# Products of a tile of ones, read by nothing, ahead of 55 waits of TensorE in a four-layer network on one core

## The reference

```python
xn = _layernorm(x, axis=-1)
x = x + _L0_attn_ref(xn, ...) + _L0_ffn_ref(xn, ...)   # causal attention, 16 heads; ternary weights
xn = _layernorm(x, axis=-1)
x = x + _L1_attn_ref(xn, ...) + _L1_ffn_ref(xn, ...)   # gated recurrence; 16 experts, top 2, + shared
xn = _layernorm(x, axis=-1)
x = x + _L2_attn_ref(xn, ...) + _L2_ffn_ref(xn, ...)   # one head of 256; weights from a spline
xn = _layernorm(x, axis=-1)
x = x + _L3_attn_ref(xn, ...) + _L3_ffn_ref(xn, ...)   # rotary attention, 16 heads; 8 experts, top 2
return x
```

## Time and profile before

| | |
|---|---|
| median of 3 runs | 1212.69 us (1212.25 to 1215.65) |
| the profiled execution's own time | 1219.58 us |
| its span, first to last instruction | 1218.0 us |
| PE busy | 1096.1 us, 90% of the span |
| mean granted clock of TensorE | 0.951 |

### The profile page before, as it was taken

One profiled execution on the slowest core, in us unless ns is written; L12 is line 12 of the kernel. 1 busy time (PEld: TensorE's weight loads), 2 busy tenths in 40 slices (PEclk: granted clock), 3 DMA queues, 4 the chain that ended last, 5 costly groups with the idle time before them and its releaser, 6 DMA issues.

```text
span 1218.0 us, 17428 instructions
## 1 busy us (share of the span) xinstructions
PE 1096.1 (90%) x6542; PEld 720.0 (59%) x6556; DVE 841.0 (69%) x1602; ACT 641.5 (53%) x980; POOL 498.2 (41%) x549
## 2 busy tenths in 40 slices
PE   3698999999999888999579999999699998997998
PEld 2466686766665454674257998989234543553445
DVE  6985856678568897955767435267877679668751
ACT  6644647466569885642135333242187166465473
POOL 4864748375524526411774052244231331141131
PEclk9778999999999999998789999999799989998999
DMA  7724344324340101267370000006914526425320
GB/s 216 214 55 146 87 129 149 116 79 142 94 174 35 36 1 48 70 198 229 106 75 27 1 1 1 1 10 159 217 38 122 140 55 149 101 67 155 92 72 18
DMA packets 86116, 116.42 MB, mean 96 GB/s; under 512 B 29617, under 2 KB 43281, under 8 KB 85265
## 3 DMA queue, kind: packets, MB, share of 16 engines
q1 hardware_dynamic: 47792, 70.28, 19.2%
q0 software_dynamic: 38240, 45.03, 15.1%
HBM read 81.54 MB, written 40.40 MB: 100 GB/s over the span
## 4 chain that ended last, share of the span: by engine, by line
PE 61%; DVE 14%; ACT 7%; POOL 6%; issue 6%; DMA 5%; SPq 1%; ACTq 0%; DVEq 0%; POOLq 0%
PE pair L693 23%; PE bank L693 18%; PE bank L772 6%; PE pair L762 5%; PE pair L751 4%; DVE max L1157 3%; POOL gathered L2092 2%; ACT probs L1681 2%; DMA h<-comb 1%; PE pair L712 1%; PE bank L780 1%; SPq L2124 1%; POOL h L2110 1%; PE pair L792 1%; DMA kept<-q_low 1%
## 5 line engine op out<-in xcount | busy, mean ns | idle before, releaser
L1157 DVE TENSOR_REDUCE max<-pair 128x2 f32<-128x1024 f32 (+3 forms) x256 | 252.5, 1021 | 61.7 <-PE pair L742 32.1
L1681 ACT ACTIVATE probs<-pair 128x1024 f32<-128x1024 f32 (+3 forms) x256 | 212.5, 865 | 103.3 <-PE pair L762 85.6
L751 PE MATMUL pair<-ks,qs 64*128 64x512 f32 (+3 forms) x512 | 110.6, 456 | 24.4 <-DVE max L1157 10.8
L2013 POOL TENSOR_TENSOR h_low<-hidden,h_high 128x512 fp32r<-128x512 f32 x64 | 82.8, 1299 | 97.8 <-ACT h_high L1719 97.3
L772 PE MATMUL bank<-probs,v 128*32 128x512 f32 (+3 forms) x1024 | 115.4, 536 | 1.1 <-POOL probs L2057 0.5
L762 PE MATMUL pair<-qs,ks 64*128 64x512 f32 (+3 forms) x512 | 102.1, 435 | 13.3 <-DVE max L1157 5.1
L751 PEld LDWEIGHTS pair<-ks,qs 64*128 64x128 f32 x512 | 50.4, 199 | 80.3 <-DVE max L1157 31.5
L762 PEld LDWEIGHTS pair<-qs,ks 64*128 64x128 f32 x512 | 46.2, 190 | 76.7 <-ACT probs L1681 24.5
L1713 ACT ACTIVATE hidden<-pair 128x512 f32<-128x512 f32 x64 | 38.2, 599 | 80.9 <-PE pair L693 69.9
L2110 POOL TENSOR_TENSOR h<-mix_h,h 128x512 bf16<-128x512 f32 x48 | 54.9, 1172 | 57.4 <-DMA h<-comb 39.1
L1196 DVE TENSOR_TENSOR x<-bank,x 128x512 f32<-128x512 f32 x32 | 22.0, 688 | 80.2 <-PE bank L693 80.1
(11 more groups left out here) (330 smaller groups left out, 2673.9 us busy)
## 6 DMA issues: line engine op xcount, KB each, us to landing
kept<-q_high SPq DMA_DIRECT2D x64, 256.0 KB, 3.8
qs<-kept POOLq DMA_DIRECT2D x32, 512.0 KB, 4.1
ks<-kept POOLq DMA_DIRECT2D x32, 512.0 KB, 5.2
kept<-q_low SPq DMA_DIRECT2D x32, 256.0 KB, 4.1
expert_in<-in_experts_in SPq DMA_DIRECT2D x16, 352.0 KB, 4.1
expert_out<-in_experts_out SPq DMA_DIRECT2D x16, 256.0 KB, 5.5
h<-comb SPq DMA_DIRECT2D x4, 1024.0 KB, 5.5
tern_raw<-in_ffn_in SPq DMA_DIRECT2D x8, 256.0 KB, 6.6
```

Of the source, the lines that this page charges most:

```text
L751: made = mm(to[:, hh, 0:n], m.qs[k][slot][r0:r0 + STACK, p, qt * P:(qt + 1) * P], m.ks[k][slot][r0:r0 + STACK, p, 0:n], start=True, stop=k ...
L1157: V.tensor_reduce(m.max[:, g % 2, :, p, qt], to[:, :, 0:n], AX.X, ALU.max).then_inc(*s.done("top"))
L1681: A.activation(m.probs[(2 * kt + p) % 4][:, :, q0:T], to[:, :, q0:T], ACT.Exp, scale=0.25).then_inc(*s.done("exp"))
L2013: Q.tensor_tensor(m.h_low[k][:, j, :], m.hidden[k][j % 2][:, :], m.h_high[k][:, j, :].bitcast(F32), ALU.subtract).then_inc(*s.done("low"))
```

## The change

Two new kinds of PE step are put between the others. A `warm` step writes a pair, a `hum` step one bank. Each does 4 times n products of 128 columns, `ones16` by `ones16`, into PSUM, and nothing reads them: 35 groups with 197 x 4 products and 20 with 72 x 4, together 1076. A group waits until its banks are free as every step does, and then for nothing else (ones16 has long been there). `DUE` gets new numbers, since every inserted step shifts those behind it, but the order of all other steps on all five engines stays the same, and so do their banks.

```diff
+WARM = (11, 4, 5, 9, 11, 3, 4, 1, 1, 3, 7, 4, 1, 1, 2, 39, 6, 8, 7, 1, 3, 3, 2, 9, 8, 3, 10, 7, 3, 3, 3, 4, 6, 4, 1,)
+HUM = (5, 5, 9, 5, 2, 6, 5, 1, 4, 4, 5, 2, 2, 5, 2, 4, 1, 2, 2, 1,)
...
 PARTS = {
     "PE": {
+        "warm": keys(range(len(WARM))), "hum": keys(range(len(HUM))),
...
+    "warm": "2 11 15 18 21 74 468 473 487 492 502 568 571 575 597 604 606 732 736 742 744 749 752 754 757 846 849 859 861 864 866 869 873 1030 1049",
+    "hum": "6 13 71 465 475 490 601 705 707 710 714 718 720 722 725 1035 1039 1043 1047 1058",
...
-BANKS = {"tern_sum": "pair",
+BANKS = {"warm": "pair", "hum": "one", "tern_sum": "pair",
...
+    "warm": "00400402044424400442442444240204400",
+    "hum": "66767667777777777776",
...
+    "warm": lambda n: [], "hum": lambda n: [],
...
+    def warm(n):
+
+        to = bank("warm", n)
+        pe.wait_ge(*at("set_dve", 0))
+        for i in range(4 * WARM[n]):
+            made = mm(to[:, 0, i % 4 * P:(i % 4 + 1) * P], m.ones16[:, :], m.ones16[:, :], start=True, stop=True)
+        made.then_inc(*s.done("warm"))
+
+    def hum(n):
+
+        to = bank("hum", n)
+        pe.wait_ge(*at("set_dve", 0))
+        for i in range(4 * HUM[n]):
+            made = mm(to[:, i % 4 * P:(i % 4 + 1) * P], m.ones16[:, :], m.ones16[:, :], start=True, stop=True)
+        made.then_inc(*s.done("hum"))
```

More of the change, by code:

```diff
@@ L291 @@
 JOINT = {name: joint for joint, names in {
+    "idle_pe": ("warm", "hum"),
     "route_pe": ("count", "logit_turn"),
@@ L305 @@
           "gates1": 2, "rest1": 3, "qkv2": 1, "small3": 2, "bias3": 3, "qkv3": 2, "wo3": 1, "shared3": 2}
-BANKS = {"tern_sum": "pair", "turn": "pair", "qk": "pair", "vals": "pair", "score": "pair", "prob": "pair", "weigh": "acc", "back": "one",
+BANKS = {"warm": "pair", "hum": "one", "tern_sum": "pair", "turn": "pair", "qk": "pair", "vals": "pair", "score": "pair", "prob": "pair", "weigh": "acc", "back": "one",
          "rows": "pair", "unit": "pair", "down": "one", "mean": "one", "proj": "pair", "gate": "two", "gamma": "pair", "inflow_turn": "pair", "mem_turn": "two",
@@ L1022, in mix @@
         made.then_inc(*s.done("mix"))
-    parts = {"tern_sum": tern_sum, "turn": turn_x, "qk": qk, "vals": vals, "score": score, "prob": prob, "weigh": weigh, "back": back, "rows": rows, "out": out,
+    parts = {"warm": warm, "hum": hum, "tern_sum": tern_sum, "turn": turn_x, "qk": qk, "vals": vals, "score": score, "prob": prob, "weigh": weigh, "back": back, "rows": rows, "out": out,
              "unit": unit, "down": down, "mean": mean, "proj": proj, "gate": gate, "gamma": gamma, "inflow_turn": inflow_turn, "mem_turn": mem_turn, "shared": shared,
```

## The result

The change makes the kernel slower: 1225.61 us (median of 20 executions, 1219.99 to 1233.39) against 1216.96 us for the kernel before on the same chip (20 executions, 1209.89 to 1224.72). The ratio is 1.0073, 95% interval 1.0053 to 1.0093, so +8.9 us with 6.5 to 11.3. The three executions of before that the prediction knew, with a median of 1212.69, are the first of its 20. The profiled execution of after has a span of 1225.5 us, 7.5 more than before's 1218.0, and nearly the whole median difference can be followed in this pair of traces.

What follows compares the result with a forecast made beforehand. PE's work plus its waits was taken to bound the kernel; -11.9 us from A, B, D, E, F and J and +9.6 from H and I gave -2.3, so 1212.69 would become 1210.4 us, range 1203.5 to 1219.0.

Steps and rivals of the forecast that it cites:

- H: From mix (0, 4) to back (3, 0, 0): products outside the wait, partly given back by clock and waits; +5.6 us.
- I: From back (3, 0, 0) to turn (3, 2): 8.4 us of products, partly given back by clock and idle time; +4.0 us.
- rival of ones without effect: Products of ones do nothing for the clock and nothing comes back: about +18 us, 1231 us; chance 0.04.
- slower rival: Nothing of H, I and J lies in a wait: +7.6 us, 1220.3 us; chance 0.18.
- J: From turn (3, 2) to the end: products mostly in waits, DVE limits the gain from the clock; -1.2 us.
- A: Start to score (0, 0, 2, 0, 3): faster transposes, then DVE sets the time and covers PE; -0.3 us.
- G: From turn (2, 3) to mix (0, 4): DVE is busy with row maxima, so faster scores only wait; 0.
- B: Up to back (0, 0, 1): products fit the wait for row maxima and PE's low-clock work shortens; -2.3 us.
- E: Up to merge (0): 10.20 us of low-clock work halves and the gathers start earlier; -4.7 us.
- C: Between back (0, 0, 1) and expert_out (3), ahead of D: ACT is busy and hides PE; 0.
- D: Up to expert_out (3): products fit two waits and two low-clock windows full of PE work shorten; -3.1 us.
- F: From merge (0) to turn (2, 3): 156 products fill half a wait, the clock falls again under the gathers; -0.3 us.

Runs made afterwards that it cites:

- k1: The kernel before with its 32 indirect gathers as plain reads of the same bytes (result not the network's): 1213.52 us, ratio 0.9936.
- e3: The whole change, but each of the 16 groups of H and I has 4 products in place of 4 to 40: 1226.67 us, ratio 1.0012 to before.
- e1: The change without the 320 products of H and I, the other 39 groups kept: 1221.80 us, ratio 0.9976 to the kernel before.
- e2: Only the 320 products of H and I, none of the change's other 39 groups: 1241.51 us, ratio 1.0131 to the kernel before.
- h1: The kernel before, unchanged, run again for a profile: 1229.49 us, one execution.
- g2: The change without H, I and the 156 products ahead of the transposes of turn (2, 0): 1217.42 us, ratio 0.9934 to the kernel before.
- h2: g2 also without warm 1 to 4, 116 products where DVE sets the time: 1220.14 us, ratio 0.9974 to the kernel before.
- h4: h2 with group I, 156 products, put back: 1229.18 us, ratio 1.0045 to the kernel before.

## Why the prediction was wrong

**The clock came as forecast; the price of the ones in H and I was too low.** Products of ones do raise the clock (0.951 to 0.983, "about 0.98" was forecast), at 0.056 us each (0.054). The Trainium skill, "TensorE: Matmul & The Clock Gate", section "Wait — 56ns, not 53.3ns?", gives about 62 ns per MATMUL where the sequencer's own program decodes it, and 55.6 ns from start to start for products of 128 columns at the full clock. The trace's 0.0559 us agrees with the second, and no run here shows the first. The Trainium skill, same page, Part 1, has activity release the throttle; the mean clock of 0.983 agrees, even for products that nothing reads. The rival of ones without effect is out. The forecast of -2.3 became +7.5 in the pair. Of the 15.2 us between 1210.4 and the 1225.61 measured, 4.3 are the base: the median of the kernel before is 1216.96 over 20 executions, where the first three had 1212.69. The slower rival had +7.6, by the mechanism that the traces show ("nothing of H, I and J lies in a wait"), and I gave it 0.18. That its number meets the pair's is luck: it had 18.3 for H, I and J and -10.7 for the rest, and the pair has 14.4 and -6.9.

**I: +4.0 forecast, +7.9 measured** (8.7, 9.0 and 10.3 in the other pairs). Two terms of the step failed. The first is "where PE is idle for 2.3 us", half of it taken as room for products. It is mostly waits of 0.84, 0.53 and 0.55 us for DVE and ACT (timeline of PE, before):

```profile
977.44 0.50 PE L762 MATMUL pair<-qs,ks 64*128 64x512 f32 x2 [0.84 <-DVE max L1157]
979.07 0.79 PE L751 MATMUL pair<-ks,qs 64*128 64x512 f32 x2 [0.53 <-ACT probs L1681]
...
989.83 0.49 PE L751 MATMUL pair<-ks,qs 64*128 64x512 f32 x2 [0.55 <-DVE mix_h L1547]
```

Each is a round trip: PE's product, the maximum, the exponential or the `mix_h` that reads it, PE's next product. What is put ahead of the product moves the whole trip. The idle time is then as long as before, which the windows show to 0.04 us. The second term is the clock, which I let give back 3.2 us: of the products' 8.7 us, 7.9 were paid, so it gave 0.8, and this term is 2.4 of the 3.9 us. One stretch of 3.4 us at 0.50 was left, 981.8 to 985.2, partly under the group's own products.

**H: +5.6 forecast, +6.6** (10.7 and 8.9 without gathers). Here I saw that the group stands behind the wait; 32 products at the half clock took 3.25 us as forecast (3.5). I had taken the low end of my own bounds, +5.6 of +5.6 to +10.6. The waits absorbed 1.3 us, not 1.8, and the clock gave back some 2.7, not 3.2 (10.6 of products, less 1.3, less the 6.6 paid). My figure for the clock holds only where it was low before; in k1 it wasn't, and there all is paid.

**A to G: -10.7 forecast, -6.9 in the pair, -14.5 without gathers.** B was right (-2.7, forecast -2.3), E too (-4.4, forecast -4.7; the gathers of the earlier trace rows start at 582.64, 6.5 us earlier and not 10). C with D gave -0.5 for -3.1: the clock is at 0.50 again at 473.2 to 476.6, behind the filled wait. Against k1 the two gave -3.4 and E -7.0, but k1's own low stretches in D were 6.8 us each and that of E 13.7, where the kernel before had 3.5, 3.4 and 10.2. So these gains go with how long the clock happened to stay down in the execution that one compares with, by 2.9 us for C and D and 2.6 for E. F cost 1.3 where I had -0.3: the second half of the wait (8.71 us) let the clock fall, as forecast, and the transposes still took 1.94 us. In A, DVE, busy for 9.84 of 10.20 us, did not cover PE as I held: with warm 1 to 4 unit (0, 0, 1) ends 2.4 us earlier. Most of it is lost again between 55 and 60 us, where the next low stretch begins; why isn't shown. So the -0.6 at the end of A is near my -0.3 by luck.

**J: -1.2 forecast**, -0.1 in the pair and -1.2 without gathers.

The error of 9.8 us in the pair is so 3.9 of I, 1.0 of H, 1.1 of J and 3.8 of A to G.

**All profiles together** tell more than the pair, as each stretch can be measured in every trace. The stretch of H is 57.0 to 60.4 us long in the six kernels with the whole group and 49.0 to 53.4 in the eleven without: +7.9 on average, where I had +5.6. The stretch of I is 69.5 to 71.8 us in six and 58.9 to 64.3 in eleven: +9.1, where I had +4.0 (e3, with its short groups, has 51.5 and 61.5). J is -0.7. The first gather starts at 578.8 on average in the eleven profiles with all of A to E and at 588.8 in the four without: the ten us of the forecast, though the pair shows 6.5. So A to E held, and H and I cost 17.0 us, not 9.6; that is the loss. The averages are over profiles of several chips, and -10.0 + 17.0 - 0.7 = +6.3 us leaves out F and G.

## What to carry to other kernels

Before filling an engine's idle time, ask who ends each wait: one that ends with another engine's answer to this engine's own product moves along and absorbs nothing, so look in the trace for waits for a transfer or for long work of another engine on something else. A raised clock pays only where the slowed engine set the time, and a group of fillers is paid at once if it stands one step behind its wait. The version with A to G, J and 44 products ahead of mix (0, 5), without H, I and warm 15 (g4), beats both kernels: 0.9929 (0.9907 to 0.9951) of the time of the kernel before, where the change has 1.0108 on the same chip (g1).

## What was not expected of the hardware

In twelve of the fourteen profiles with gathers, PE's work came late while the indirect gathers ran, 9 to 16 us from the first gather to mix (0, 4). In ten, instructions of PE came late, at whatever instruction was next: 0.70 us per instruction for 36 instructions in e1 (587 to 612). In e2 and h1, and beside the late instructions in g2 to g4 and h2 to h4, a semaphore of PE rose 10 to 17 us behind the modelled end of its product. The program of the change has the halt in g1 and not in its first profile, the kernel before has it in h1 and not in its first profile, and no fixed place in PE's program brings it (h2). Products of ones ahead of the gathers aren't needed, as e2 and h1 have none. With plain reads it was absent in four profiles of four, and the kernel before gained 0.64%. The gathers also issue slower (16 in 20 us; 16 plain reads in 8.6), so the gain is not all the halt's, and whether it is the indirect addressing or this pace that matters wasn't tried. Gathers are needed for the halt as far as these runs go, but don't suffice: the first pair has them and no halt. How an engine's work comes late at all stays open. The Trainium skill, "Runtime: NRT & Kernel Launch", section "Instruction fetch mechanics", says that instructions stream in blocks of 256; the queue of instruction blocks agrees, 52 of them before and 60 after for 2152 more instructions. In e1 no block of this queue moved during the halt, and the next, at 614.57, took 0.93 us: no slow block held PE, though one asked for late isn't excluded.
